# A two-layer vision kernel whose scan rows carry a second layer: gate multiplied on VectorE, output projection after the step sizes, a new table of rows

## The reference

```python
# layer 0
xn = rmsnorm(x, norm_w)                                   # per token, over channels
def mamba(x):                                             # run on xn and on the flipped xn
    u, z = split(x @ in_proj_w.T)
    u = silu(causal_conv1d(u, 4 taps) + b)
    dt, Bm, Cm = split(u @ x_proj_w.T, [24, 40])
    delta = softplus(dt @ dt_proj_w.T + dt_proj_b)        # per channel and token
    h = exp(delta * A) * h + delta * u * Bm               # scan over 1024 tokens, 16 states
    y = sum_n(h * Cm) + u * D
    return (y * silu(z)) @ out_proj_w.T
g = (mamba(xn) + flip(mamba(flip(xn)))) * scale_mod
local = sigmoid(depthwise_conv3x3(xn) + dw_b) * xn
x = x + res_scale * (g + local)
# layer 1, on tokens
t = t + causal_attention(layernorm(t)) @ Wo               # 6 heads of 64
t = t + gelu(layernorm(t) @ kron(c_fc_1, c_fc_2).T) @ kron(c_proj_1, c_proj_2).T
```

## Time and profile before

| | |
|---|---|
| median of 3 runs | 4873.35 us |
| profiled execution, its own time / its span | 4890.22 us / 4887.8 us |
| busy share PE, DVE, ACT, POOL | 72%, 75%, 51%, 55% |
| granted clock of TensorE, mean | 0.829 |
| DMA queue of POOL / of SP, share of 16 engines | 45.4% / 22.7% |
| b_row and c_row loads, issue to landing | 5.5 and 4.8 us |
| y additions, issue to landing | 6.9 us |

### The profile page before, as it was taken

One profiled execution on the slowest core, in us unless ns is written; L12 is line 12 of the kernel. 1 busy time (PEld: TensorE's weight loads), 2 busy tenths in 40 slices (PEclk: granted clock), 3 DMA queues, 4 the chain that ended last, 5 costly groups with the idle time before them and its releaser, 6 DMA issues.

```text
span 4887.8 us, 40273 instructions
## 1 busy us (share of the span) xinstructions
PE 3535.2 (72%) x11626; PEld 1778.8 (36%) x11626; DVE 3651.7 (75%) x2769; ACT 2488.6 (51%) x3507; POOL 2712.4 (55%) x1652
## 2 busy tenths in 40 slices
PE   6300977687885878758877687767887587877797
PEld 2100335323452235513354133542345323452372
DVE  4899669797687867887687976979768786789221
ACT  3433446455564545545565544645556454565262
POOL 1787446575565655655565744656556565567100
PEclk9655989878887889878888798987888788987898
DMA  3999468786686776875677856878667676679200
GB/s 89 225 247 246 97 148 184 176 199 159 138 182 164 187 167 142 193 169 147 161 179 170 199 145 150 181 178 203 144 144 179 164 190 165 146 180 207 64 6 13
DMA packets 224022, 785.08 MB, mean 161 GB/s; under 512 B 25293, under 2 KB 40959, under 8 KB 223519
## 3 DMA queue, kind: packets, MB, share of 16 engines
q0 software_dynamic: 117504, 427.87, 45.4%
q1 hardware_dynamic: 106270, 354.32, 22.7%
HBM read 339.60 MB, written 39.85 MB: 78 GB/s over the span
## 4 chain that ended last, share of the span: by engine, by line
PE 32%; DVE 24%; issue 19%; DMA 11%; POOL 8%; ACT 5%; DVEq 0%; SPq 0%; ACTq 0%; POOLq 0%
DVE pBC L1130 14%; PE pW L451 10%; DMA y<-hb 8%; PE pW L556 6%; POOL hb L1309 6%; DVE stat L1170 3%; PE pW L636 3%; PE pW L613 3%; DMA area<-in_x 2%; ACT prob L947 1%; DVE du_f L1105 1%; PE pW L535 1%; PE pW L521 1%; PE pW L489 1%; PE pW L661 1%
## 5 line engine op out<-in xcount | busy, mean ns | idle before, releaser
L1130 DVE TENSOR_TENSOR_SCAN pBC<-pBC,hb 128x1024 f32<-128x1024 f32 x768 | 1756.9, 2288 | 413.5 <-ACT pBC L780 270.6
L1323 POOL DMA_DIRECT2D y<-hb x792 | 753.7, 955 | 1080.0 <-DVE hb L1139 1005.8
L1309 POOL TENSOR_TENSOR hb<-du_f,b_row 128x1024 f32<-128x1024 f32 x384 | 996.8, 2604 | 63.3 <-DMA y<-hb 53.2
L1309 POOL TENSOR_TENSOR hb<-uc_b,b_row 128x1024 f32<-128x1024 f32 x384 | 1007.4, 2629 | 37.8 <-DMA y<-hb 37.0
L1139 DVE TENSOR_TENSOR hb<-pBC,c_row 128x1024 f32<-128x1024 f32 x768 | 940.5, 1225 | 44.7 <-DVE pBC L1130 0.5
L780 ACT ACTIVATE pBC<-xres,vec 128x1024 f32<-128x1024 f32 x384 | 428.3, 1118 | 388.2 <-DVE hb L1139 387.4
L636 PE MATMUL pW<-area,pt 128*128 128x64 f32 x3456 | 437.6, 281 | 152.5 <-ACT pt L937 152.5
L780 ACT ACTIVATE pBC<-delta,vec 128x1024 f32<-128x1024 f32 x384 | 428.6, 1117 | 196.4 <-DVE hb L1139 196.3
L636 PEld LDWEIGHTS pW<-area,pt 128*128 128x128 f32 x3456 | 408.9, 194 | 209.8 <-ACT pt L937 201.5
L1170 DVE TENSOR_REDUCE stat<-pW 128x1 f32<-128x640 f32 (+7 forms) x361 | 257.8, 751 | 260.8 <-PE pW L559 260.1
L947 ACT ACTIVATE prob<-pW,stat 128x640 f32<-128x640 f32 (+7 forms) x361 | 265.6, 744 | 194.8 <-DVE stat L1170 194.8
(11 more groups left out here) (163 smaller groups left out, 4808.8 us busy)
## 6 DMA issues: line engine op xcount, KB each, us to landing
y<-hb POOLq DMA_DIRECT2D x792, 512.0 KB, 6.9
b_row<-bc_rows SPq DMA_DIRECT2D x256, 512.0 KB, 5.5
c_row<-bc_rows SPq DMA_DIRECT2D x256, 512.0 KB, 4.8
area<-in_x SPq DMA_DIRECT2D x8, 1536.0 KB, 13.0
kept_residual<-in_x SPq DMA_DIRECT2D x8, 1536.0 KB, 18.1
kept_residual<-du_f POOLq DMA_DIRECT2D x24, 512.0 KB, 5.4
xres<-kept_residual SPq DMA_DIRECT2D x8, 1536.0 KB, 14.9
out_x<-xa SPq DMA_DIRECT2D x8, 1536.0 KB, 7.6
```

What stands on the lines that cost most here:

```text
L1130: dve.tensor_tensor_scan(flow(d, buf), flow(d, buf), flow(d, hb[slot(r)][:, :]), 0.0, ALU.mult, ALU.add).then_inc(scan_done, 1)
L1309: pool.tensor_tensor(hb[q % NHB][:, :], du[d][:, k, :], b_row[g % 2][:, :], ALU.mult)\
L1323: pool.dma_start(y[:, k, :], hb[q % NHB][:, :], accum_op=ALU.add).then_inc(y_in[k], 16)
```

## The change

- `gated`: y times silu(z) moves from POOL, where it was written to y, to DVE behind the depthwise steps, and is written to zs. `out_project` reads zs.
- `out_project` stands wholly behind the three step sizes, uses four PSUM banks instead of two, and `finish` moves into rows 0, 1 and 3.
- The depthwise convolution is done channel group by channel group, into prob, hb4 and hb3 instead of du_f; its third sigmoid stands ahead of the softplus, which is now done group by group.
- Row 0's decay stands ahead of the skip terms, the third of which moves behind row 0.
- Both layer norms keep mean and variance in banks 0 and 1, beside the step sizes and the next sample's projection in banks 2 and 3, and their rstd is one Ln and one Exp over both banks.
- The table of rows: the second direction's preparation about 8 rows later, each score group with one row of its own (rows 32 to 61, but 42 and 52), the next sample's projection in rows 70 to 72 instead of 94 and 95.

```diff
-R0, R1 = 15, 66
-RS = 12
-STEPS = ([("step_z", n, n) for n in range(3)] + [("step_u", 0, 4), ("step_u", 1, 7), ("step_bc", 0, 9)]
-         + [("step_skip", k, 9 + k) for k in range(KT)]
-         + [(kind, k, 15 + 2 * k + more) for k in range(KT) for kind, more in (("step_in", 0), ("step_sum", 1), ("step_copy", 2))])
+RS = 18
+STEPS = ([("step_y", 2, 0)] + [("step_z", n, (5, 7, 8)[n]) for n in range(3)]
+         + [("step_u", 0, 10), ("step_u", 1, 14), ("step_bc", 0, 18)] + [("step_skip", k, RS - KT + k) for k in range(KT)]
+         + [(kind, k, 23 + 3 * k + i) for k in range(KT)
+            for i, kind in enumerate(("step_in", "step_log", "step_sum", "step_copy"))])
+FINISH = [("finish", t, (0, 0, 1, 1, 3, 3)[t]) for t in range(6)]
+Q0, S0, S1 = 24, 32, 63
...
+def attention():
+
+    return [(kind, p, S0 + p * (S1 - S0) // (NG + 1)) for p in range(NG + 1) for kind in ("scores", "values")]
...
+    + norm(1, S1 + 5, 2) + [("next_in", t, S1 + 7 + t // 2) for t in range(6)]
...
-        gate = du_f
+        gate = [prob[:, :], hb[4][:, :], hb[3][:, :]]
...
         def out_bank(t):
 
-            return pW[:, 2 + t % 2, :]
+            return pW[:, (t + 2) % 4, :]
...
-                    if t >= 2:
-                        pe.wait_ge(xa_ready, at(6, b, t - 1))
-                    project(out_bank(t), op_w, slice(128 * m, 128 * m + 128), y,
+                    if t in (2, 3) and not (isinstance(b, int) and b == NB - 1):
+                        pe.wait_ge(delta_ready, at(6, b + 1, 3))
+                    elif t >= 4:
+                        pe.wait_ge(xa_ready, at(6, b, t - 3))
+                    project(out_bank(t), op_w, slice(128 * m, 128 * m + 128), zs,
...
-                    if layer1:
-                        out_project(b - 1, 0, 2)
                     for k in range(KT):
                         step_size(b, 0, k)
                     if layer1:
-                        out_project(b - 1, 2, 6)
+                        out_project(b - 1, 0, 6)
...
                     gates(b, 0, 2)
                     narrow_copies(b, 0)
+                    gates(b, 2, 3)
                     act.preload_act_table_set(LOG_EXP)
                     for k in range(KT):
                         soft_abs(b, 0, k)
-                    for k in range(KT):
                         soft_exp(b, 0, k)
-                    for k in range(KT):
                         soft_log(b, 0, k)
-                    gates(b, 2, 3)
-                    act.preload_act_table_set(LOG_EXP)
-                    for k in range(KT):
+                    decay(b, 0)
+                    for k in range(2):
                         skip(b, 0, k)
-                    decay(b, 0)
...
+            def gated(b):
+
+                for k in range(KT):
+                    dve.wait_ge(y_in[k], at(YIN, b, YIN))
+                    dve.wait_ge(zs_ready, at(3, b, k + 1))
+                    dve.tensor_tensor(zs[:, k, :], y[:, k, :], zs[:, k, :], ALU.mult).then_inc(yz_ready, 1)
...
-                    depthwise(b, 0, 22)
+                    depthwise(b, 0, 20)
                     local(b, 0)
-                    depthwise(b, 22, 24)
+                    depthwise(b, 20, 22)
                     local(b, 1)
-                    depthwise(b, 24, 27)
+                    depthwise(b, 22, 27)
+                    if layer1:
+                        gated(b - 1)
+                    local(b, 2)
                     for k in range(KT):
-                        if k == 2:
-                            local(b, 2)
-                        elif layer1:
-                            finish(b - 1, k)
                         soft_sum(b, 0, k)
                         times_u(b, k)
-                    if layer1:
-                        for t in range(2, 6):
-                            finish(b - 1, t)
...
-                    for k in range(KT):
-                        pool.wait_ge(y_in[k], at(YIN, b, YIN))
-                        pool.wait_ge(zs_ready, at(3, b, k + 1))
-                        pool.tensor_tensor(y[:, k, :], y[:, k, :], zs[:, k, :], ALU.mult).then_inc(yz_ready, 1)
```

More of the change, by code:

```diff
@@ L63, with norm @@
 NFG = NF // FGRP
-FRONT = ([("proj", t, 2.0 if t < 12 else 1.6) for t in range(NPJ)]
-         + [x for p in range(NG + 1) for x in (("scores", p, 3.7), ("values", p, 3.7))]
-         + [("ctx_t", g, 0.8) for g in range(6)] + [("next_square", 0, 0.0)] + [("wo", t, 2.0) for t in range(6)])
-R0, R1 = 15, 66
-RS = 12
-STEPS = ([("step_z", n, n) for n in range(3)] + [("step_u", 0, 4), ("step_u", 1, 7), ("step_bc", 0, 9)]
-         + [("step_skip", k, 9 + k) for k in range(KT)]
-         + [(kind, k, 15 + 2 * k + more) for k in range(KT) for kind, more in (("step_in", 0), ("step_sum", 1), ("step_copy", 2))])
-def norm(n, r):
-    return [("ln_mean", n, r), ("ln_xc", n, r + (2 if n == 0 else 1))] + [
-        (kind, n, r + (3 if n == 0 else 2) + i) for i, kind in enumerate(("ln_var", "ln_rs", "ln_apply"))]
+RS = 18
[5 more added lines that the diff above has]
+Q0, S0, S1 = 24, 32, 63
+def norm(n, r, gap):
+    return [("ln_mean", n, r)] + [
+        (kind, n, r + gap + i) for i, kind in enumerate(("ln_xc", "ln_var", "ln_rs", "ln_apply"))]
 def mlp(c, r):
@@ L83, in mlp @@
         ("mlp", c * (NFG + 1) + NFG, r + 2 * NFG), ("mlp_out", c, r + 2 * NFG), ("mlp_add", c, r + 2 * NFG + 1)]
[L86 to L102, removed]
+def attention():
+    return [(kind, p, S0 + p * (S1 - S0) // (NG + 1)) for p in range(NG + 1) for kind in ("scores", "values")]
+PLAN = sorted(
+    norm(0, 18, 2) + [("proj", t, Q0 + t * (S0 - Q0) // NPJ) for t in range(NPJ)] + attention()
+    + [("ctx_t", t, S1 + t // 3) for t in range(6)] + [("wo", t, S1 + 2 + t // 3) for t in range(6)]
+    + [("wo_add", t, S1 + 3 + t // 2) for t in range(6)]
+    + [("next_square", 0, S1 + 4), ("next_mean", 0, S1 + 4), ("next_rstd", 0, S1 + 5), ("next_norm", 0, S1 + 6)]
+    + norm(1, S1 + 5, 2) + [("next_in", t, S1 + 7 + t // 2) for t in range(6)]
+    + [("mlp_in", 0, S1 + 11), ("mlp_split", 0, S1 + 12)] + mlp(0, S1 + 13) + mlp(1, S1 + 23), key=lambda x: x[2])
+SLOTS = [[(kind, n) for kind, n, row in STEPS + FINISH + PLAN if row == r] for r in range(ROWS)]
+NEXT = ("next_square", "next_mean", "next_rstd", "next_norm", "next_in")
 CROWDED = [n for n in range(1, NG + 1) if any({("values", n - 1), ("scores", n)} <= set(row) for row in SLOTS)]
@@ L868, in item @@
                 a = b - 1
-                if kind == "step_z" and not early:
+                if kind == "step_y" and not early:
+                    skip(b, 0, n)
+                elif kind == "step_z" and not early:
                     copy_z(b, 6 + 2 * n)
@@ L885, in item @@
                     soft_exp(b, 1, n)
+                elif kind == "step_log" and not early:
                     soft_log(b, 1, n)
@@ L981, in item @@
                         act.activation(xsq[:, k, :], xnext[:, k, :], ACT.Square).then_inc(sq_ready, 1)
-                elif kind == "next_mean" and not early:
+                elif kind == "next_rstd" and not early:
                     act.wait_ge(ms_ready, at(2, b + 1, 2))
@@ L1143, in item @@
                 a = b - 1
-                if kind == "step_sum" and not early:
+                if kind == "finish" and not early:
+                    finish(a, n)
+                elif kind == "step_sum" and not early:
                     soft_sum(b, 1, n)
@@ L1181, in item @@
                     dve.reciprocal(stat[:, 2, st:st + nt], stat[:, 1, st:st + nt]).then_inc(rinv_ready, 1)
-                elif kind == "wo" and n and not early or kind == "wo_last" and not early:
-                    t = n - 1 if kind == "wo" else 5
-                    m, c = t // 2, t % 2
+                elif kind == "wo_add" and not early:
+                    t, m, c = n, n // 2, n % 2
                     toks = slice(c * HALF, (c + 1) * HALF)
@@ L1202, in item @@
                     dve.tensor_tensor(xa[:, :, toks], xa[:, :, toks], pW[:, 0:3, :], ALU.add).then_inc(x2_ready, 1)
[L1203 to L1206 removed]
                 elif kind == "next_norm" and not early:
[L1209 to L1210 removed]
+                    dve.wait_ge(wo_ready, at(6, b, 0))
+                    for border in (up[:, :, 0:NTAP - 1], up[:, :, UP - NTAP + 1:UP],
+                                   xnp[:, :, 0, :], xnp[:, :, HH + 1, :], xnp[:, :, 1:1 + HH, 0:1],
                                    xnp[:, :, 1:1 + HH, WW + 1:WP]):
```

101 lines of the change are left out of this document (55 added, 46 removed).

## The result

The changed kernel takes 4761.0 us (median of 4 runs, 4750.0 to 4767.5) where the kernel before, on the same chip, takes 4875.2 (4872.5 to 4886.8): ratio 0.976, 95% interval 0.973 to 0.979. The forecast was 4773.

What follows compares the result with a forecast made beforehand. DVE was taken to set the end where nearly full, idle 122 of 577.2 us a period, with PE pacing projections. Six periods at -15.9 gave -95, with the rest -100 against 4890, less 17 for the median: 4773, range 4700 to 4815.

Steps and rivals of the forecast that it cites:

- The prologue: Between samples: one dependent depthwise chain of 42.2 us, then sigmoid, table load, softplus and DVE's last operations, 56.7 us.
- A: The stretch without rows, prologue of the next sample: 56.7 us where 79.5 stood, 22.8 less.
- The stall at row 18: DVE waits for the B row load held up in SP's queue: 12.6 to 24 us, taken as 17; 12 in sample 0.
- rival 2: At row 18: the stall isn't there, ACT or the DMAs being far earlier; 131 us less, 4642; chance 0.12.
- B: Rows 0 to 23 after the change: 115 us, with rows, norm and `finish` at 94.3 and the stall at 17.
- C: Rows 24 to 31, with the 20 projections: PE sets the time, 65 us instead of 69.6.
- D: Rows 32 to 62, with 26 score groups at one row: PE's chain at 5.8 us a group, 169.3 instead of 190.7.
- E: Rows 63 to 95: 155.3 us instead of 168.3, DVE idle 18 instead of 31.3, 7 left of the x load wait.
- The sum outside the period: Outside the six loop periods: first and last samples' rows, prologues and last gate multiply; with the periods' -95, together -100 us.
- Rival 1: Rows 32 to 61: score groups stay at today's 7.06 us each; 229 us more, 5002; chance 0.14.
- rival 3: At row 18: the stall is at its upper end; +49 us, 4822; chance 0.15 with what lies up to no change.
- rival 4: Whole period: the other stretches give back what the prologue gains; no change, 4873; chance 0.08.

Runs made afterwards that it cites:

- Number 9: Against the changed kernel, the output projection's first two tiles go ahead of the step sizes, as in the kernel before: 4829.3 us, ratio 0.989.
- number 5: Against the changed kernel, the gate multiplication goes back to POOL, still writing into z's buffer: 4787.6 us, ratio 0.980.
- numbers 1 and 2: Against the changed kernel: 1 issues row loads for rows 18 to 23 before the store and two weights, 4704.9 us; 2 moves only the weights behind them, 4721.0 us.

## Why the prediction was right, point by point

- **The prologue**: right in kind and size. The chain is three first operations and 24 dependent steps at 1.31, then softplus, then rows. Number 9 shows that putting the step sizes first is worth 10.5 us a period, and number 5 that the gate on DVE is worth 4, not the 10 that the earlier trace rows suggested. Wrong: that the 5.9 us where the loop returns stay. They are 1.4 to 1.8, 4.5 us a period on the good side. No run was made on the cause, and the profile names no releaser in either kernel: open. The other 7 of A's 26 us were not taken apart.
- **The stall at row 18**: there, in the row named, 16.4 against 17. With R the start of row 17 (620.98), the copies ended at R + 4.4, not R + 6.8, the B row went out at R + 6.5, not R + 8, and was used 11.0 us after its issue, where the ends of the forecast allowed 5.5 and 17. The 17 was a choice between 12.6 and 24, and its nearness is partly luck. Its working was right only in part. SP's block and the weights account for 10 of it by numbers 1 and 2; the step that failed is the statement that row 18 "without this would start at R + 3.5". Without it the row starts 6.5 us later than that, behind the additions, and I had put 1 us for them. So the stall's price was right, what lifting it is worth was not: rival 2's 131 us are not to be had, 56 were. The rule of the Trainium skill ("DMA: Bandwidth & Descriptors", section "Queues, rings and completion order") gave 15.5; the trace has 16.4, between it and my 17, and does not decide. The terms of B (94.3 + 2 + 1 + 17) add up to 114.3, not to the 115 that I put; measured 112.2.
- **C**: 65 against 66.2, bound by PE as said; its spread of 8 us with the clock was not in the sum.
- **D**: 169.3 against 169.3, but by two errors that cancel. The groups are 5.55 apart, not 5.8 (26 x 0.25 = 6.5 less), and each of the two empty rows costs 17.2 - 11.1 = 6.1 on top of its groups, not the 2.45 that 8.25 allowed (7 more), for the clock. The 17.2 are the time from the maximum ahead of the empty row to the second one behind it (785.25 to 802.49), 11.1 two groups at 5.55.
- **E**: 155.3 against 160.4. The load wait is 8.95, not 7, since it landed 14 us after its issue and not 13, the copies cost 7.8 as said (8), the rest is small waits and 2 us more of DVE's own work. In samples 2 to 6 the load took 16 to 17 us to land and the wait is 10.8 to 12.1: the mean E is 162.9.
- **The sum outside the period**: the six periods gained 117 us in the profiles, not 95, because the period I took, the first, is the shortest of the kernel before (577.2; the others are 580.4 to 583.6). The last sample's rows became 0.9 longer, not 16, sample 0's rows 3.7, not 9; the prologue of sample 1 gained 19.1, as said, the first prologue 2.9 (4 forecast) and the end 4.9 (1 forecast). That is 139.6 in the profiles, where the forecast had 100. It is 114 in the medians, since the profiled run of before lies 15.0 us above its median (4890.2 against 4875.2) and that of after 11.0 below. The forecast took a profile of before for its start and took off 17 for the median; that after would fall the other way could not be known, and that 4773 came within 12 us of 4761 is in part luck.

Rival 1 is excluded by the 5.55, rival 2 by the row at 640.95, rival 3 by its 16.43, rival 4 by the windows: the gain of A was not given back as a whole, DVE's idle time fell by 19 us in the period.

## What to carry to other kernels

Walk every in-order queue, the one that only issues DMAs too, past each step that a change moves: here one wait of SP held up the row loads behind it, and it showed in no line of the diff. A row left empty to give a chain time can cost more than its own length, because here TensorE paused in it and came back at half its clock: fill the rows and put the spare ones beside work that is bound elsewhere. And removing a stall is worth only what the next limit leaves: find that one before counting the whole of it.
